# Slot attention stages of a mamba hybrid: two phases per stage, outputs as 64-row matmuls, repeated transposes in the GRU chain

## The reference, cut to what matters

```python
x = x + mamba(layernorm(x))          # two layers, final norm with weights
x = x + slot_block(layernorm(x))     # stage f1 of the kernel
x = x + window_attention(layernorm(x))
x = x + slot_block(layernorm(x))     # stage f2

def slot_block(x):                   # 64 slots, top 8
    S = slot_init * slot_scale       # [64, 256], same for each of the 2 sequences
    h = gelu(concat(x, mean(S)) @ w1.T + b1)          # 128 hidden
    logits = (h @ w2.T + b2) / (abs(tau) + 0.1)       # 64 slots
    alpha = softmax over the 8 largest, 0 elsewhere   # [tokens, 64]
    gi = (alpha.T @ x) / (alpha.sum(tokens) + 1e-8)   # per sequence
    r, z, n = GRU gates of (gi, S);  S1 = (1 - z) * n + z * S
    return (alpha @ (S1 @ wv.T + bv)) @ wo.T + bo
```

## Time and profile before

| | us |
|---|---|
| median of three runs | 2516.12 (2514.9 to 2517.61) |
| profiled execution, its time and its span | 2518.79, 2517.0 |
| f1: first instruction, end of last gather, first output matmul, last addition's end | 1786.57, 1921.36, 1934.37, 1949.07 |
| attention's first instruction | 1953.62 |
| f2: the same four | 2399.05, 2482.13, 2495.42, 2512.47 |
| idle of TensorE ahead of L1284, L1288, L1297, L1303, L1312 | 0.95, 0.47, 2.57, 0.75, 1.06 |
| busy over the span: TensorE, VectorE, ScalarE, GpSimd | 87%, 75%, 72%, 64% |

### The profile page before, as it was taken

One profiled execution on the slowest core, in us unless ns is written; L12 is line 12 of the kernel. 1 busy time (PEld: TensorE's weight loads), 2 busy tenths in 40 slices (PEclk: granted clock), 3 DMA queues, 4 the chain that ended last, 5 costly groups with the idle time before them and its releaser, 6 DMA issues. The chain is left out here.

```text
span 2517.0 us, 40372 instructions
## 1 busy us (share of the span) xinstructions
...
## 2 busy tenths in 40 slices
...
GB/s 169 123 106 22 118 43 93 96 32 118 42 94 87 78 118 30 114 77 51 118 16 119 66 61 111 17 118 9 190 1 62 65 33 33 29 33 25 21 116 67
DMA packets 129787, 183.73 MB, mean 73 GB/s; under 512 B 14002, under 2 KB 75954, under 8 KB 129204
## 3 DMA queue, kind: packets, MB, share of 16 engines
...
...
## 5 line engine op out<-in xcount | busy, mean ns | idle before, releaser
L624 POOL TENSOR_TENSOR h<-h,C_rep 128x512 f32<-128x512 f32 x1024 | 1275.9, 1283 | 202.4 <-ACT h_carry L530 202.4
L406 DVE TENSOR_TENSOR_SCAN h<-decay,h_carry,psum 128x512 f32<-128x512 f32 x768 | 955.8, 1270 | 126.4 <-PE psum L755 93.6
L522 ACT ACTIVATE decay<-dt_rep,A 128x512 f32<-128x512 f32 x1024 | 729.3, 713 | 103.6 <-DVE h L406 93.0
L755 PEld LDWEIGHTS psum<-ident,u_B 128*128 128x128 f32 x4096 | 479.1, 142 | 562.5 <-DVE h L406 310.3
L755 PE MATMUL psum<-ident,u_B 128*128 128x128 f32 x4096 | 632.5, 281 | 141.5 <-DVE h L406 109.4
L545 ACT ACTIVATE u_B<-u_tok,B_tok 128x512 f32<-128x512 f32 x832 | 589.0, 709 | 64.3 <-PE psum L755 46.6
L406 DVE TENSOR_TENSOR_SCAN h<-decay,zero,psum 128x512 f32<-128x512 f32 x256 | 319.0, 1271 | 57.2 <-PE psum L755 35.9
L764 PE MATMUL psum<-h,state_sum 128*32 128x512 f32 x2048 | 281.5, 623 | 11.7 <-POOL h L624 11.4
L1600 ACT ACTIVATE a_probs_T<-a_psum 128x512 f32<-128x512 f32 x128 | 76.4, 597 | 197.2 <-PE a_psum L1684 197.2
L613 POOL TENSOR_TENSOR u_B<-u_tok,B_tok 128x512 f32<-128x512 f32 x192 | 200.7, 1045 | 13.5 <-DVE u_tok L377 13.5
L1542 DVE TENSOR_REDUCE a_row_max<-a_psum 128x4 f32<-128x512 f32 x128 | 88.4, 691 | 143.3 <-PE a_psum L1675 143.3
...
...
## 6 DMA issues: line engine op xcount, KB each, us to landing
dt_rep<-dt_rows SPq DMA_DIRECT2D x256, 256.0 KB, 5.5
C_rep<-C_rows SPq DMA_DIRECT2D x256, 64.0 KB, 2.0
...
```

What stands on the lines that cost most here:

```text
L406: dve.tensor_tensor_scan(h[:, slot(u)], dec[:, u % DEC], PS[:, u % 2], first, ALU.mult, ALU.add)\
L522: act.activation(dec[:, u % DEC], dtr[:, k % EG], ACT.Exp, scale=A[:, s // STEPS, k:k + 1]).then_inc(S["decay"], 1)
L624: pool.tensor_tensor(h[:, slot(u)], h[:, slot(u)], crep[:, k // EG], ALU.mult).then_inc(S["hc"], 1)
L755: ins = pe.transpose(PS[:, u % 2, tb * P:(tb + 1) * P], pr[:, f % 2, tb, eg], ident[:])
```

## The change

- VectorE's `routing` is split. `top_k(g)` runs in the loop over the groups, now after `combine(g + 2)` instead of before it; `weigh(n)` (mask, sum, reciprocal, product) runs for all four groups after the loop. Logits, alpha, top and sums have a buffer per group; the marked logits are written in place, so the marking waits for the subtraction.
- ScalarE does all Gelus in the loop and all exponentials after it, in the order `ORDER` = 0, 2, 1, 3. In the loop `norm_x(g + 1)` and `norm_r(g + 2)` stand between `features(g)` and `hidden(g)`.
- ScalarE normalises tiles 0 to 3 of a group of x, GpSimd tiles 4 to 7 by `tensor_scalar`, in its own order: rstd of r, rstd of x, these four, then the next group.
- TensorE: `hidden(g)`, `features(g + 1)`, `logits(g)` in the loop, then `prepare_slots`, then two gathers of two groups each, one of either sequence, whose matmuls alternate between the column halves.
- `warm(n)` issues n transposes of the identity into bank 1, at five places in the GRU chain.
- Outputs: `SVo` isn't block diagonal any more. Each tile is a matmul of 64 rows and 256 columns, upper and lower rows of `aT` in turn; the tiles of upper and lower rows go to two banks, with one addition per bank.

```diff
+ORDER = [GB * b + n for n in range(GB) for b in range(BATCH)]
...
-lg = sb("logits", [P, TG, SL])
-top = sb("top8", [P, TG, TOPK])
-rest = sb("logits_without_top", [P, TG, SL])
-ex = sb("exps", [P, TG, SL])
-et = sb("top_exps", [P, TG, TOPK])
-es = sb("exp_sums", [P, 2, TG])
-al = sb("alpha", [P, 2, TG, SL])
+lg = sb("logits", [P, G, TG, SL])
+top = sb("top8", [P, G, TG, TOPK])
+al = sb("alpha", [P, G, TG, SL])
+et = sb("top_exps", [P, G, TG, TOPK])
+es = sb("exp_sums", [P, G, 2, TG])
...
-SVo = sb("slot_out", [P, BATCH, 2, D])
+SVo = sb("slot_out", [P, BATCH, D])
...
-    for n in range(PER * G):
-        rstd(n)
-        if n == PER:
-            pool.memset(SVo[:], 0.0).then_inc(S["zeros"], 1)
+    def norm_x(g):
+        n = PER * g + PER - 1
+        pool.wait_ge(S["nm"], n + 1)
+        for i in range(HG_, TG):
+            pool.tensor_scalar(xn[:, TG * g + i, 0:D], xa[:, TG * g + i], rs[:, n, i:i + 1], nm[:, n, i:i + 1],
+                               ALU.mult, ALU.add).then_inc(S["xn_p"], 1)
+    for g in range(G):
+        for n in range(PER * g, PER * (g + 1)):
+            rstd(n)
+        norm_x(g)
...
-    def routing(g):
+    def top_k(g):
         dve.wait_ge(S["l_mm"], g + 1)
-        dve.scalar_tensor_tensor(lg[:], PS[:, 6].rearrange("p (i s) -> p i s", s=SL), rt[:, 3:4],
+        dve.scalar_tensor_tensor(lg[:, g], PS[:, 6].rearrange("p (i s) -> p i s", s=SL), rt[:, 3:4],
                                  b2[:].rearrange("p (i s) -> p i s", i=1).to_broadcast([P, TG, SL]),
...
+        dve.tensor_tensor(al[:, g], lg[:, g], top[:, g, :, 0:1].to_broadcast([P, TG, SL]), ALU.subtract)\
             .then_inc(S["shift"], 1)
-        dve.tensor_tensor(et[:], top[:], top[:, :, 0:1].to_broadcast([P, TG, TOPK]), ALU.subtract)\
+        dve.tensor_tensor(et[:, g], top[:, g], top[:, g, :, 0:1].to_broadcast([P, TG, TOPK]), ALU.subtract)\
             .then_inc(S["shift"], 1)
+        dve.wait_ge(S["shift"], 2 * g + 1)
         for i in range(TG):
-            dve.match_replace(rest[:, i], top[:, i], lg[:, i], NEG).then_inc(S["rest"], 1)
+            dve.match_replace(lg[:, g, i], top[:, g, i], lg[:, g, i], NEG).then_inc(S["rest"], 1)
+    def weigh(n):
+        g = ORDER[n]
         dve.wait_ge(S["rest"], TG * (g + 1))
-        dve.wait_ge(S["ex"], 2 * g + 1)
-        dve.scalar_tensor_tensor(ex[:], rest[:], NEG, ex[:], ALU.is_equal, ALU.mult).then_inc(S["mask"], 1)
-        dve.wait_ge(S["ex"], 2 * g + 2)
-        dve.tensor_reduce(es[:, 0], et[:], AX, ALU.add).then_inc(S["es"], 1)
-        dve.wait_ge(S["es"], 2 * g + 1)
-        dve.reciprocal(es[:, 1], es[:, 0]).then_inc(S["es"], 1)
-        dve.wait_ge(S["es"], 2 * g + 2)
-        dve.wait_ge(S["mask"], g + 1)
-        if g >= 2:
-            dve.wait_ge(S["slot_mm"], g - 1)
-        dve.tensor_tensor(al[:, g % 2], ex[:], es[:, 1].rearrange("p (i o) -> p i o", o=1).to_broadcast([P, TG, SL]),
+        dve.wait_ge(S["ex"], 2 * n + 1)
+        dve.scalar_tensor_tensor(al[:, g], lg[:, g], NEG, al[:, g], ALU.is_equal, ALU.mult).then_inc(S["mask"], 1)
+        dve.wait_ge(S["ex"], 2 * n + 2)
+        dve.tensor_reduce(es[:, g, 0], et[:, g], AX, ALU.add).then_inc(S["es"], 1)
+        dve.wait_ge(S["es"], 2 * n + 1)
+        dve.reciprocal(es[:, g, 1], es[:, g, 0]).then_inc(S["es"], 1)
+        dve.wait_ge(S["es"], 2 * n + 2)
+        dve.wait_ge(S["mask"], n + 1)
+        dve.tensor_tensor(al[:, g], al[:, g],
+                          es[:, g, 1].rearrange("p (i o) -> p i o", o=1).to_broadcast([P, TG, SL]),
                           ALU.mult).then_inc(S["alpha"], 1)
...
     for g in range(G):
-        routing(g)
         combine(g + 2)
+        top_k(g)
         if normed:
             r_moments(g + 3)
-    dve.wait_ge(S["slot_mm"], G)
+    for n in range(G):
+        weigh(n)
...
-    dve.wait_ge(S["zeros"], 1)
     for b in range(BATCH):
+        dve.tensor_tensor(SVo[:, b], PS[:, 6, b * D:(b + 1) * D], hb[:, 1], ALU.add).then_inc(S["SVo"], 1)
+    for m in range(NT // HG_):
+        four = xa[:, HG_ * m:HG_ * (m + 1)].rearrange("p (j i) d -> p i j d", i=2)
         for i in range(2):
-            h = slice(SL * i, SL * (i + 1))
-            dve.tensor_tensor(SVo[h, b, i], PS[h, 6, b * D:(b + 1) * D], hb[h, 1], ALU.add)\
-                .then_inc(S["SVo"], 1)
-    for n in range(NT // 2):
-        dve.wait_ge(S["o_mm"], n + 1)
-        dve.tensor_tensor(xa[:, 2 * n:2 * n + 2], PS[:, n % 8].rearrange("p (i d) -> p i d", d=D),
-                          xa[:, 2 * n:2 * n + 2], ALU.add).then_inc(S["y"], 1)
+            dve.wait_ge(S["o_mm"], 2 * m + i + 1)
+            dve.tensor_tensor(four[:, i], PS[:, 2 * (m % 4) + i].rearrange("p (j d) -> p j d", d=D), four[:, i],
+                              ALU.add).then_inc(S["y"], 1)
 @block.scalar
...
     def norm_x(g):
         if g < G:
-            normalise(PER * g + PER - 1, xn, xa, g, "xn")
+            n = PER * g + PER - 1
+            act.wait_ge(S["nm"], n + 1)
+            for i in range(HG_):
+                ins = act.activation(xn[:, TG * g + i, 0:D], xa[:, TG * g + i], ACT.Identity, bias=nm[:, n, i:i + 1],
+                                     scale=rs[:, n, i:i + 1])
+            ins.then_inc(S["xn"], 1)
...
-    norm_x(1)
-    norm_r(2)
     for g in range(G):
-        features(g + 1)
+        features(g)
+        norm_x(g + 1)
+        norm_r(g + 2)
+        hidden(g)
+    for g in ORDER:
         act.wait_ge(S["shift"], 2 * g + 1)
-        act.activation(ex[:], ex[:], ACT.Exp).then_inc(S["ex"], 1)
+        act.activation(al[:, g], al[:, g], ACT.Exp).then_inc(S["ex"], 1)
         act.wait_ge(S["shift"], 2 * g + 2)
-        act.activation(et[:], et[:], ACT.Exp).then_inc(S["ex"], 1)
-        hidden(g + 1)
-        act.wait_ge(S["a_tp"], g + 1)
-        act.activation(aT[:, HG_ * g:HG_ * (g + 1)].rearrange("p i t -> p (i t)"), PS[:, 5], ACT.Copy)\
-            .then_inc(S["aT"], 1)
-        norm_x(g + 2)
-        norm_r(g + 3)
+        act.activation(et[:, g], et[:, g], ACT.Exp).then_inc(S["ex"], 1)
     act.wait_ge(S["pre_mm"], 1)
     act.activation(hb[:].rearrange("p a d -> p (a d)"), PS[:, 1], ACT.Copy).then_inc(S["pre"], 1)
     act.wait_ge(S["wvo_mm"], 1)
     act.activation(wvo[:].rearrange("p k d -> p (k d)"), PS[:, 3], ACT.Copy).then_inc(S["wvo"], 1)
+    for n in range(G):
+        g = ORDER[n]
+        act.wait_ge(S["a_tp"], n + 1)
+        act.activation(aT[:, HG_ * g:HG_ * (g + 1)].rearrange("p i t -> p (i t)"), PS[:, 4 + n % 2], ACT.Copy)\
+            .then_inc(S["aT"], 1)
     act.wait_ge(S["g_tp"], 1)
...
-            pe.wait_ge(S["xn"], 2 * g + hf + 1)
+            if hf == 0:
+                pe.wait_ge(S["xn"], g + 1)
+            else:
+                pe.wait_ge(S["xn_p"], HG_ * (g + 1))
...
-        if g >= 2:
-            pe.wait_ge(S["aT"], g - 1)
         for hf in range(2):
             pe.wait_ge(S["xnT"], 4 * g + 2 * hf + 2)
+            if g:
+                pe.wait_ge(S["hT"], 2 * (g - 1) + hf + 1)
...
-    def gather(g):
-        b = g // GB
-        pe.wait_ge(S["alpha"], g + 1)
-        pe.wait_ge(S["hT"], min(2 * (g + 2), 2 * G))
-        for i in range(HG_):
-            ins = pe.transpose(PS[:, 5, i * P:(i + 1) * P],
-                               al[:, g % 2, 2 * i:2 * i + 2].rearrange("p i s -> p (i s)"), ident[:])
-        ins.then_inc(S["a_tp"], 1)
+    def gather(n):
+        for j in range(BATCH):
+            g = ORDER[BATCH * n + j]
+            pe.wait_ge(S["alpha"], BATCH * n + j + 1)
+            if n:
+                pe.wait_ge(S["aT"], j + 1)
+            for i in range(HG_):
+                ins = pe.transpose(PS[:, 4 + j, i * P:(i + 1) * P],
+                                   al[:, g, 2 * i:2 * i + 2].rearrange("p i s -> p (i s)"), ident[:])
+            ins.then_inc(S["a_tp"], 1)
         for i in range(TG):
-            ins = pe.matmul(PS[SL * b:SL * (b + 1), 7, 0:D + 1], al[:, g % 2, i], xn[:, TG * g + i],
-                            start=(g % GB == 0 and i == 0), stop=(g % GB == GB - 1 and i == TG - 1))
+            for b in range(BATCH):
+                g = ORDER[BATCH * n + b]
+                ins = pe.matmul(PS[SL * b:SL * (b + 1), 7, 0:D + 1], al[:, g, i], xn[:, TG * g + i],
+                                start=(n == 0 and i == 0), stop=(n == GB - 1 and i == TG - 1))
         ins.then_inc(S["slot_mm"], 1)
+    def warm(n):
+        for _ in range(n):
+            pe.transpose(PS[:, 1, 0:P], ident[:], ident[:])
...
-    hidden(0)
-    logits(0)
     for g in range(G):
+        hidden(g)
         features(g + 1)
-        hidden(g + 1)
-        logits(g + 1)
-        if g == G - 1:
-            prepare_slots()
-        gather(g)
+        logits(g)
+    prepare_slots()
+    pe.wait_ge(S["hT"], 2 * G)
+    pe.wait_ge(S["pre"], 1)
+    for n in range(GB):
+        gather(n)
+    warm(6)
...
     ins.then_inc(S["g_tp"], 1)
+    warm(3)
...
+    warm(16)
...
+    warm(5)
...
-    pe.wait_ge(S["SVo"], 2)
-    for n in range(NT // 2):
```

(20 more changed lines are left out.)

25 lines of the change are left out of this document (9 added, 16 removed).

## The result

The changed kernel takes 2478.73 us (median of 4, 2477.72 to 2479.87) beside 2516.35 of the kernel before: ratio 0.9851, 95% interval 0.9834 to 0.9868. The profiled execution took 2478.56 for a span of 2476.8, which is 40.2 less than the span of before; the one of before had been 2.4 over its median, and the table goes by the spans. The long part of a stage is the time from its first instruction to the end of its last gather.

A forecast was written before the change was run, and what follows sets the result against it. The prediction took the slot stages' loops to wait on themselves, with no engine full; 15.5 + 2.7 + 2.0 + 2.3 + 1.5 + 3.9 = 27.9 us off 2516.1 gave 2488.2, range 2479 to 2501.

The forecast's parts named there:

- Prices: Both slot stages: costs per group read from profile rows, such as ScalarE's normalisation of 8 tiles 4.04 us, top-k 4.3.
- 1: Half of x's normalisation goes to GpSimd at 1.225 us a tile: 0.8 us late per group, 0 when hidden.
- 1 and 2, first stage: First slot stage to its last gather, split normalisation and two phases: loop period 24.3 instead of 26.2 us, -2.7.
- 2, second stage: Second slot stage to its last gather, exponentials out of the loop: end at 2466.6 instead of 2482.13, -15.5 us.
- 2, gathers: Gathers at the stage's end: column halves run at once, 1.1 + 3.5 us each, two 9.2 and not 16.1.
- 3, chain: GRU chain: repeated transposes hold TensorE's full clock, and one addition less: -2.0 and -2.3 us.
- rival B: GRU chain and outputs: the transposes don't hold the clock, 2492.7 us; chance 0.1.
- 4, outputs: Output parts: 64-row matmuls with row halves at once, so the stores bound them: -1.5 and -3.9 us.
- A: Outputs: the row halves don't run at once, 3.0 us less gain, 2491.2 us; chance 0.1.
- E: Outputs: each change of row half empties the array, slower by 7.4, 2523.5 us; chance 0.04.
- Rival C: Slot stages: the SBUF port's lock also makes VectorE wait for GpSimd's tiles, 11 us, 2499 us; chance 0.1.
- Rival D: Slot stages: GpSimd's tiles fall between VectorE's operations (-4), TensorE warm throughout the second (-3), 2481 us; chance 0.09.

The follow-up runs named there:

- e1: The changed kernel with GpSimd's normalisation tiles written as (x - mean) * rstd instead of x * rstd + shift: 2493.26 us, ratio 0.9898.
- e5: The changed kernel with each gather's records issued one column half after the other instead of in turn: 2489.06 us, ratio 0.9886.
- e3: The changed kernel without its repeated transposes (36 per stage): 2481.25 us, ratio 0.9862.
- e4: The changed kernel with the outputs as before, 16 matmuls of 128 rows by 512 columns: 2483.17 us, ratio 0.9864.
- e8: The changed kernel with VectorE's first-stage addition of the residual's bias waiting for GpSimd's shift of r: 2469.95 us, ratio 0.9813.

## Why the prediction was off

The direction, most mechanisms and four of the eight parts were right; the size was 9.7 short by the medians. The step that failed is the price of GpSimd's tile in Prices and 1, 1.225 us where 0.545 was measured. In f1 a top-k counted in the wrong period came on top. Attention's 3.5, for which the sum had nothing, is luck. By the prediction's own steps:

- *Prices*: GpSimd's tile at 1.225 was wrong, it is 0.55. I took the row with the same shape and operand kinds and passed over the pair of operations: (subtract, mult) there, (mult, add) here. e1 puts it at 7.4 and 7.5 us, the largest error, with what the late tiles do to the clock included. For the unseen operation I should have bounded the price from both sides instead of taking an equal-looking row as the row.
- *1 and 2, first stage*: L1002 came 88.2 after the stage's start in the forecast and at 82.8. By e1 (85.65) the tile's price makes 2.9 of the 5.5. Of the other 2.6 the first L1002, which I had 1.1 later than even e1, and a slip make up all: I gave the first period a top-k (4.3) that stands only in the second, while the moments of r stand in both. 20.7 against 24.0, and 22.6 in e1; the second period, 24.2 against 24.3, was right, the lock of L999 included. That the slip makes the difference is read from the timeline and was not tried.
- *2, second stage*: 65.1 against 67.6, a small error made of two of opposite sign: 7.5 too dear for the tile, and 5 too cheap for the last group, which I had run at the full clock although TensorE idles ahead of it (e1: 3.51 and 6.22). That a sum comes near says little of its terms.
- *2, gathers*: 3.5 each forecast, 3.70 and 5.38 measured. Column halves run at once (e5); the fall of the clock in a busy engine was not in the prediction, +1.7 per stage.
- *3, chain*: right, 1.9 and 2.2 for 2.0 and 2.3. The transposes hold the clock (e3); rival B is out.
- *4, outputs*: right, 1.4 and 3.8 for 1.5 and 3.9, bound by the stores (e4). Rivals A and E are out: 0.45 for a pair.
- *Rival C*: out. In the changed kernel's slot stages a two-tensor operation of VectorE beside GpSimd's tiles is longer by 0.25 at most (0.42 instead of 0.17 at 1835.34, 0.88 instead of 0.69 at 2408.33), and a tile is 0.55. The other direction is what costs, and the Trainium skill ("SBUF — State Buffer", "Summary: rules for kernel authors") says that of the two the second to issue waits for the whole of the first: the trace agrees, with a power of 3.61 us beside L999 and of 1.64 without it. That is 2 us a period, and e8 takes it away. I had seen the row, put the lock into the period, and not asked what it would give to move the addition.
- *Rival D* named both sources of the surplus (tiles between VectorE's operations, a warmer TensorE) at 2481 with 0.09. The range's low end of 2479 was D minus 2; attention's 3.5, in which before and after differ by luck, had no place in it, and without them, by the profiles, the time would have lain inside. The profile of before had three slow projections out of four, the worst case seen, and that could have been read there.
